# Loading the first expert matrices on 128 partitions, and the first token sort's steps spread wider

## The reference

```python
logits = xt @ Wr + br                       # xt: the normalised tokens, (2048, 128)
probs, idx = top_k(softmax(logits), 2)
probs = probs / probs.sum(axis=-1, keepdims=True)
h = einsum('td,edf->etf', xt, W1) + b1[:, None, :]      # W1 (8, 128, 512), b1 (8, 512)
h = _layernorm(relu(h), g1, be1)
y = einsum('etf,efd->etd', h, W2) + b2[:, None, :]
y = _layernorm(relu(y), g2, be2)
gate = (one_hot(idx, 8) * probs[..., None]).sum(axis=1)
out = einsum('te,etd->td', gate, y)         # x = x + tanh(g_ffn[1]) * out
```

## Time and profile before

| | us |
|---|---|
| median of three runs | 1987.57 |
| lowest and highest of them | 1983.64, 1988.05 |
| the profiled execution | 1982.25 |
| its span, first to last instruction | 1980.5 |
| PE busy | 1669.0 (84%) |
| DVE busy | 1171.3 (59%) |
| ACT busy | 772.9 (39%) |
| POOL busy | 752.7 (38%) |

### The profile page before, as it was taken

One profiled execution on the slowest core, in us unless ns is written; L12 is line 12 of the kernel. 1 busy time (PEld: TensorE's weight loads), 2 busy tenths in 40 slices (PEclk: granted clock), 3 DMA queues, 4 the chain that ended last, 5 costly groups with the idle time before them and its releaser, 6 DMA issues. The chain is left out here.

```text
span 1980.5 us, 30824 instructions
## 1 busy us (share of the span) xinstructions
PE 1669.0 (84%) x10277; PEld 1111.9 (56%) x10277; DVE 1171.3 (59%) x3054; ACT 772.9 (39%) x1957; POOL 752.7 (38%) x976
## 2 busy tenths in 40 slices
PE   6500465998999999999999997869999999999999
PEld 5400353776576555765557655445765565655656
DVE  6600367678675756757567575466757645564654
ACT  2200212443564555645556454315645622222222
POOL 3100536344475645747457475003656400000000
PEclk7855656999999999999999998979999999999999
DMA  5002101221000000000000000000000264734452
GB/s 192 25 25 80 35 2 36 77 70 39 10 7 1 1 1 6 7 1 1 1 6 7 1 1 1 0 1 1 1 1 1 68 198 118 208 117 136 133 162 86
DMA packets 63708, 92.48 MB, mean 47 GB/s; under 512 B 10952, under 2 KB 29000, under 8 KB 62784
## 3 DMA queue, kind: packets, MB, share of 16 engines
q1 hardware_dynamic: 61504, 86.31, 14.0%
q0 software_dynamic: 2048, 4.20, 0.7%
HBM read 80.51 MB, written 9.96 MB: 46 GB/s over the span
## 5 line engine op out<-in xcount | busy, mean ns | idle before, releaser
L1620 POOL TENSOR_TENSOR rows<-rows,rinv 128x512 f32<-128x512 f32 x192 | 198.7, 1064 | 117.4 <-DVE rinv L1860 117.4
L2531 ACT ACTIVATE region_b<-psum 128x512 f32<-128x512 f32 x132 | 78.8, 597 | 257.7 <-PE psum L2493 257.7
L1784 ACT ACTIVATE rows<-psum,nmax 128x512 f32<-128x512 f32 x192 | 130.0, 683 | 123.4 <-DVE nmax L1853 123.3
L2505 PEld LDWEIGHTS psum<-region_c,region_b 128*128 128x128 f32 x1024 | 132.1, 192 | 56.5 <-issue 43.8
L2569 DVE TENSOR_TENSOR region_b<-region_b,psum 128x512 f32<-128x512 f32 x128 | 87.8, 686 | 127.9 <-ACT region_b L2531 125.7
L1852 DVE TENSOR_REDUCE lg<-psum 128x2 f32<-128x1024 f32 x128 | 155.6, 1216 | 3.2
L1969 POOL TENSOR_TENSOR rows<-rows,rinv 128x128 f32<-128x128 f32 (+2 forms) x192 | 127.4, 686 | 76.4 <-DVE rinv L2138 76.4
L2133 DVE TENSOR_REDUCE nmax<-psum 128x1 f32<-128x128 f32 (+3 forms) x256 | 113.5, 485 | 41.6 <-PE psum L2015 40.5
L1864 DVE COPY turned<-psum 128x512 f32<-128x512 f32 x128 | 88.2, 689 | 80.4 <-PE psum L1680 79.5
L1668 PE MATMUL psum<-region_a,region_b 64*128 64x256 f32 x1024 | 130.6, 391 | 6.0 <-ACT rows L1784 2.9
L2505 PE MATMUL psum<-region_c,region_b 128*128 128x128 f32 x1024 | 133.5, 275 | 1.9 <-DVE region_b L2577 1.9
(11 more groups left out here) (747 smaller groups left out, 3600.9 us busy)
## 6 DMA issues: line engine op xcount, KB each, us to landing
pt<-gates SPq DMA_DIRECT2D x128, 128.0 KB, 3.0
ysb<-gates SPq DMA_DIRECT2D x128, 128.0 KB, 3.7
region_a<-in_eg SPq DMA_DIRECT2D x32, 256.0 KB, 3.4
region_a<-in_eu SPq DMA_DIRECT2D x32, 256.0 KB, 3.5
region_c<-in_weights SPq DMA_DIRECT2D x32, 256.0 KB, 4.6
sorted<-kctx SPq DMA_DIRECT2D x2, 1536.0 KB, 12.8
region_b<-sorted SPq DMA_DIRECT2D x12, 256.0 KB, 3.2
made<-rows SPq DMA_DIRECT2D x12, 256.0 KB, 2.4
```

Of the source, the lines that this page charges most:

```text
L1620: nc.gpsimd.tensor_tensor(row(u, j), row(u, j), rinv[:, 2 * u + j:2 * u + j + 1].broadcast_to([P, S]), ALU.mult).then_inc(s.pn, 1)
L1784: nc.scalar.activation(row(u, j), s_bank(u, j), ACT.Exp, bias=nmax[:, 2 * u + j:2 * u + j + 1], accum_out=sum_column(u // T, u % T, j)).th ...
L2505: mm = nc.tensor.matmul(bank(7)[:, P * t:P * (t + 1)], htb[:, i % 2, P * t:P * (t + 1)], wd, start=(i == 0 and t == 0), stop=(i == n_items ...
```

## The change

Three edits. The matrices and the copies of their last row are loaded on all 128 partitions, and the subtraction runs on 128 partitions, so that partition 127 of `w1` becomes zero. The load of the bias row into partition 127 is moved from block 1 to SP's queue of block 2, behind the waits for that block's inputs, and SP waits there for 32 instead of 16. And `route_1` of block 2 gets `step(n) = 2n` and `per_step = 4`: its pieces are due at steps 0, 2, 4, 6, 8, 10, 12, 14, 16 and 18, and the scatters at steps 20 to 27.5, two to a step.

```diff
--- before.py
+++ after.py
@@ -426,11 +426,9 @@
 
         def load_first_matrices(sp, s):
 
-            lo = early_at["b1"][0]
             for e in range(E8):
-                sp.dma_start(w1[0:D - 1, e, 0:F1], a["w1"][0:D - 1, e, :]).then_inc(s.w1_in, 16)
-                sp.dma_start(last_row(e)[0:D - 1, :], a["w1"][D - 1:D, e, :].broadcast_to([D - 1, F1])).then_inc(s.w1_in, 16)
-            sp.dma_start(w1[D - 1:D, :, 0:F1], a["early"][0:E8, lo:lo + F1].rearrange("(o e) f -> o e f", o=1)).then_inc(s.w1_in, 16)
+                sp.dma_start(w1[:, e, 0:F1], a["w1"][:, e, :]).then_inc(s.w1_in, 16)
+                sp.dma_start(last_row(e), a["w1"][D - 1:D, e, :].broadcast_to([D, F1])).then_inc(s.w1_in, 16)
 
         def clear_sorted(sp, s):
 
@@ -594,9 +592,8 @@
                 for e in range(E8):
                     yield 20 + e
                     if e == 0:
-                        pool.wait_ge(s.w1_in, 16 * (2 * E8 + 1))
-                    rows = w1[0:D - 1, e, 0:F1]
-                    nc.gpsimd.tensor_tensor(rows, rows, last_row(e)[0:D - 1, :], ALU.subtract)
+                        pool.wait_ge(s.w1_in, 16 * 2 * E8)
+                    nc.gpsimd.tensor_tensor(w1[:, e, 0:F1], w1[:, e, 0:F1], last_row(e), ALU.subtract)
 
             return record(tensor=tensor, vector=vector, scalar=scalar, gpsimd=gpsimd)
 
@@ -2629,14 +2626,17 @@
             def sync(sp):
                 sp.wait_ge(sf.inputs, 5 * 16)
                 sp.wait_ge(sg.inputs, 5 * 16)
+                lo = early_at["b1"][0]
+                sp.dma_start(w1[D - 1:D, :, 0:F1],
+                             a["early"][0:E8, lo:lo + F1].rearrange("(o e) f -> o e f", o=1)).then_inc(sw.table_in, 16)
                 lo = at["be2"][0]
                 sp.dma_start(be2_rows[:, :, :], over(a["weights"][0:E8, lo:lo + D], 0, [P, E8, D])).then_inc(sw.table_in, 16)
-                sp.wait_ge(sw.table_in, 16)
+                sp.wait_ge(sw.table_in, 32)
                 sp.wait_ge(scattered_1[0], 16 * K1 * GT)
                 for q in range(3):
                     load_pages(sp, s_pages, q)
             block_of(k, sync, front(sf, 2, bank(0), front_1, set_f),
-                     [front(sg, 3, bank(1), front_2, front_w2), route_1(sr, 0, bank(2), lambda n: n, 2)], first_loads)
+                     [front(sg, 3, bank(1), front_2, front_w2), route_1(sr, 0, bank(2), lambda n: 2 * n, 4)], first_loads)
 
         def moe_1_pages():
             k = next_block()
```

## The result

| | before | after |
|---|---|---|
| median, us | 1986.92 (4 runs, 1983.64 to 1988.05) | 1861.07 (4 runs, 1859.38 to 1868.11) |
| ratio | 1 | 0.9376, 95% interval 0.9349 to 0.9403 |
| profiled execution, span | 1982.25, 1980.5 | 1862.18, 1860.4 |
| end of block 1 | 232.37 | 112.90 |
| inputs of block 2 landed | 241.09 | 121.22 |

The change takes 125.9 us off by the medians and 120.1 by the two profiles. Forecast were 120 less, 1865, in a range of 1854 to 1878. By blocks: block 1 -119.5 (forecast -123.3), the wait for inputs -0.4, block 2 -2.5 (forecast +3.4), the rest +2.3 (forecast 0). The total is right to 0.2%, and part of that is luck: in the two profiles three errors of 2 to 6 us cancel. By the medians the gain is 6 us more than forecast.

The account below looks back on a forecast made before the run. POOL's 127.8 us wait for loads running on one DMA engine was taken as the bound. Block 1 -123.3 and block 2 +3.4 gave -119.9, so 1985 - 120 = 1865 us, range 1854 to 1878.

Parts of the forecast that it names:

- the rest: From the end of block 2 (355 us) to the end of the span: carried over unchanged, 0 us.
- Fast price: New 128-partition loads, broadcasts included, run at 423 GB/s or half of it: 10 to 20 us for 4.2 MB.
- hidden, with 2.7 us to spare: Block 1: POOL's four subtractions end at 75.8 us, before DVE's L989 ends at 78.42, so they cost nothing.
- the head: Block 2 up to the last normalisation, with route pieces twice as far apart: -9.4, -2.4, +3.35 and +2.4, sum -6.0 us.
- f2: The side front of batch 3 in block 2; its L951 was forecast at 279.2 instead of 288.59 us, -9.4.
- Step 9: Route piece in block 2, 2.44 us on DVE: -2.4 at its old place between the two L951, +2.4 at step 18.
- Six scatters "just hidden": Block 2, before POOL's first L1038: six scatters take 7.8 us and fit POOL's idle 8.02 us.
- Ten scatters at 1.45 us: Block 2, singly between POOL's sixteen softmax operations: 30.7 us against 17.8, +12.9 us.
- The tail: From POOL's last softmax operation to the end of block 2: 6.0 us instead of 9.5, -3.5 us.
- block 2 gains: Rival: POOL's small gaps and PE's higher clock take up ten scatters, -5 to -8, total 1857 to 1860; chance 11%.
- The slower rivals: Block 1 loads: 128 partitions reading the same 2 KB are served one by one; at 25 us each, 2010 us; chance 1%.
- The broadcasts on one engine: Rival, block 1: w1 pieces get fast, eight broadcasts keep 10.5 us each, ready at about 107 us, total 1897; chance 3%.

Follow-up runs that it names:

- The loads only: The changed kernel with the old steps of `route_1`, so only the loads and the moved bias row differ from the kernel before: 1864.49 us, ratio 0.9394.
- owners late: The changed kernel with only the page owners and shares of `route_1` moved from step 18 to step 21: 1864.6 us, ratio 0.9371.
- the second profile: The changed kernel, unaltered, run again on another chip beside the kernel before: 1867.65 us, ratio 0.9388.
- four late: The changed kernel with POOL's first four subtractions waiting for DVE's normalisations and the last four behind both softmaxes of block 1: 1857.7 us, ratio 0.9349.

## Why the prediction was right, point by point

**What bounds the kernel: right.** One set of loads on one DMA engine, and POOL waiting for it. The loads only give -119.2 in block 1 and the whole gain.

**The added loads: right.** Fast price for both kinds, the last landed at 42.8 us (forecast 42 to 52), no wait at L596. The clearing of `sorted` was issued at 33.0 and not near 45; nothing hung on it. That a broadcast is as fast as a plain load, taken from the `be2` row, held: both kinds land at the same pace.

**Block 1: the mechanism right, one term missed.** The step that failed is the one that calls the four subtractions "hidden, with 2.7 us to spare". I asked whether POOL would be in time for DVE and not what POOL's work does to the work of DVE beside it. 4.95 instead of 1.11 us is 3.8, and the block lost just that: -119.5 in place of -123.3; without it 109.30 instead of the 109.1 of the sum. The evidence stood in my own rows: L1115 took 3.53 us for eight in the earlier trace rows beside POOL's products, which is 0.44 each, and 2.14 without them. I had read that as DVE's normal price. The Trainium skill, "SBUF — State Buffer", section "Who interferes with whom", says that a `tensor_scalar` of DVE can take a port that it shares with GpSimd, and that whoever comes second is blocked for the whole instruction. The trace agrees: each of the four DVE instructions lasts as long as one of POOL's (1.24 and 1.23 us).

**Block 2, the head: right in sign, too small.** -9.4 was forecast for f2's first L951, and it was -12.1. I had added up what the route's products took at half clock and DVE's wait, and left out that the moved DVE work gets cheaper too (3.53 to 2.14). That is 1.4 of the 2.7 us; the other 1.3 are not traced. At POOL's first softmax operation it was -9.3 for a forecast of -6.0. Step 9 for 2.4 us was about right, as owners late showed with 3.0.

**Six scatters "just hidden": right**, with 0.04 us between them and L986.

**Ten scatters at 1.45 us: too dear.** They lengthen the stream by 10.6 us and not 12.9. I took the price of a scatter behind another operation in block 3 (1.48), where an idle 0.3 us and a longer first instruction are in it; in the tight stream it is 0.17 idle and 0.98. The lower end that I had named, 1.26, was the nearer one.

**The tail: right within its spread.** Forecast -3.5, measured -3.8 in one profile and -2.2 in the other.

**Block 2 in all.** +3.4 forecast, -2.5 measured, 0 in the second profile (113.44 against 113.64). Of the 5.9 us of error 3.3 are the head (-9.3 for -6.0), 2.3 the scatters (+10.6 for +12.9) and 0.3 the tail. The rival "block 2 gains" named the direction, with -5 to -8. Of its reasons the scatters are cheaper than I had put them; that PE's higher clock has a part in the head isn't shown, since L1069, seen at the full clock, now starts 0.8 us behind f2's first L948.

**The rest: 0 was put too surely.** It moves by several us from one execution to the next, and the forecast gave it no spread of its own. +3.8, -5.9, -0.4 and +2.3 add up to -0.2, which is why the sum of the profile sits so near: that is luck.

**The slower rivals.** 128 readers of one row cost nothing that can be seen. The broadcasts on one engine gave 1910 in one run, not 1897.

## What to carry to other kernels

When a wait of an engine goes, look not only at what it will be late for but at which of another engine's instructions its work now falls beside: a GpSimd operation of 1.23 us made each DVE normalisation beside it cost 1.24 instead of 0.28, and a wait of 1.3 us on the idle side won 3.6. Where a load of 127 partitions is slow, fill all 128 or cut it in two, here 112 and 15, and remember that one slow load holds up every fast one behind it on its queue. Small pieces that may run anywhere belong into an engine's gaps, each counted: the same sixteen scatters cost 28.4 or 19.1 us of POOL's stream by their place alone.

## What the hardware showed that I had not expected

- DVE's L1000, which reads two tiles, started 0.25 us into a scatter and did not get its turn behind it: it lasted 3.12 us, over the rest of the scatter and two whole L1040, and ended 0.3 us after the last of them. In the version with four late the same line of the source (L1001 there) met subtractions in a row and lasted 1.53 us: it ended 0.3 us after one of them and did not wait for the two behind it. Time lines of DVE and POOL there:

```profile
98.60 1.53 DVE L1001 SCALAR_TENSOR_TENSOR x<-pt,gate,x 128x256 f32<-128x256 f32 x1
...
97.35 2.50 POOL L597 TENSOR_TENSOR region_a<-region_a,region_c 128x512 f32<-128x512 f32 x2
99.81 2.88 POOL L597 TENSOR_TENSOR region_a<-region_a,region_b 128x512 f32<-128x512 f32 x2
```

  The Trainium skill, "SBUF — State Buffer", section "Who interferes with whom", says that a DVE instruction with two SBUF inputs contends with a GpSimd instruction that reads SBUF, and that whoever comes second is blocked while the other lasts. The second case agrees, with one subtraction. In the first it was passed over by a second instruction and a third, and the measurement decides. The L627 beside L596 went in turns.
- An indirect scatter costs POOL 0.96 us behind a scatter, with 0.30 us of issue ahead of it, and 0.98 with 0.17 behind a softmax operation.
- The same stage of the same code, PE busy throughout, took 68.6 to 76.7 us, with the granted clock between 1.00 and 0.72. Differences of under 10 us between single executions of this kernel say nothing of a change unless the blocks that it touches show them.
